# Moving the maximum's split, the scaled y and the fp8 bias to GpSimd, with all stack transfers on SyncE

## What is computed

```python
x = x + _layernorm(_L0_attn_ref(_layernorm(x), ...))   # 16 heads of 8, softmax attention, fp32
x = x + _layernorm(_L0_ffn_ref(_layernorm(x), ...))    # fp8 GEMM and a bias, bf16
x = x + _layernorm(_L1_attn_ref(_layernorm(x), ...))   # gated linear recurrence and an MLP
x = x + _layernorm(_L1_ffn_ref(_layernorm(x), ...))    # 8 experts of capacity 100
```

```python
scores = jnp.einsum('bhqd,bhkd->bhqk', q, k) / SCALING
att = jax.nn.softmax(scores, axis=-1)
...
x_q = (x.astype(jnp.float32) / s_in).astype(jnp.float8_e4m3fn)
y = jnp.dot(x_q.astype(jnp.float32), k_q.astype(jnp.float32), preferred_element_type=jnp.float32)
y = (y * (s_in * s_k)).astype(dtype) + bias
```

## Time and profile before

| | us |
|---|---|
| median of three runs (lowest, highest) | 1607.09 (1601.43, 1607.19) |
| span of the profiled execution, first to last instruction | 1596.0 |
| PE busy in it, matmul records | 1221.0 (77%) |
| DVE busy | 1231.6 (77%) |
| ACT busy | 976.0 (61%) |
| POOL busy | 839.4 (53%) |

### The profile page before, as it was taken

One profiled execution on the slowest core, in us unless ns is written; L12 is line 12 of the kernel. 1 busy time (PEld: TensorE's weight loads), 2 busy tenths in 40 slices (PEclk: granted clock), 3 DMA queues, 4 the chain that ended last, 5 costly groups with the idle time before them and its releaser, 6 DMA issues.

```text
span 1596.0 us, 25182 instructions
## 1 busy us (share of the span) xinstructions
PE 1221.0 (77%) x6480; PEld 465.6 (29%) x6480; DVE 1231.6 (77%) x2629; ACT 976.0 (61%) x1621; POOL 839.4 (53%) x1051
## 2 busy tenths in 40 slices
PE   1488888888798788798788888755887777887763
PEld 0022222222132222222222222122454444454442
DVE  2577789889779779778878887334688989989873
ACT  0067677777567677667667777434767566567630
POOL 5124355556455545545535543354377676677663
PEclk9979999999889999979989999676999999999976
DMA  2133023112202102102012020000000000000000
GB/s 42 24 81 47 19 31 48 33 15 49 48 1 47 37 12 47 31 18 47 20 29 47 8 35 2 0 1 0 1 7 7 14 7 7 13 7 7 14 7 20
DMA packets 46973, 37.10 MB, mean 23 GB/s; under 512 B 8080, under 2 KB 44816, under 8 KB 46864
## 3 DMA queue, kind: packets, MB, share of 16 engines
q1 hardware_dynamic: 42256, 29.65, 9.8%
q0 software_dynamic: 4608, 6.32, 2.5%
HBM read 6.04 MB, written 4.19 MB: 6 GB/s over the span
## 4 chain that ended last, share of the span: by engine, by line
PE 36%; DVE 22%; issue 16%; POOL 11%; ACT 8%; SPq 3%; DMA 3%; DVEq 1%; ACTq 0%; POOLq 0%
PE bank L218 13%; PE bank L202 11%; ACT probs L361 5%; DVE neg_max L505 5%; PE bank L226 3%; DVE probs L1061 3%; SPq L640 3%; DMA k_stack<-k_parts 2%; DVE probs L930 2%; PE bank_pair L189 2%; PE bank L287 2%; PE bank L749 2%; POOL probs L1171 1%; POOL rs_x L1104 1%; PE bank_pair L741 1%
## 5 line engine op out<-in xcount | busy, mean ns | idle before, releaser
L361 ACT ACTIVATE probs<-bank 128x512 f32<-128x512 f32 x1024 | 577.0, 598 | 261.0 <-PE bank L202 237.9
L505 DVE TENSOR_REDUCE neg_max<-bank_pair 128x2 f32<-128x1024 f32 x512 | 611.7, 1216 | 146.6 <-PE bank_pair L189 142.3
L202 PE MATMUL bank<-q_stack,k_stack 50*128 50x512 bf16 x1024 | 353.9, 409 | 119.6 <-ACT probs L361 119.3
L218 PE MATMUL bank<-probs,v_pad 128*32 128x512 f32 x2048 | 295.5, 652 | 0.0
L189 PE MATMUL bank_pair<-k_stack,q_stack 48*128 48x512 bf16 x1024 | 236.8, 407 | 48.0 <-DMA k_stack<-k_parts 24.8
L202 PEld LDWEIGHTS bank<-q_stack,k_stack 50*128 50x128 bf16 x1024 | 82.0, 93 | 549.4 <-ACT probs L361 487.7
L741 PE MATMUL bank_pair<-probs,w_gates 128*128 128x512 f32 x256 | 129.2, 652 | 20.5 <-DVE probs L1061 17.7
L1061 DVE SCALAR_TENSOR_TENSOR probs<-v_pad,conv_w,probs 128x512 f32<-128x512 f32 x96 | 98.1, 1061 | 6.3 <-ACT probs L893 5.6
L741 PE MATMUL bank_pair<-probs,w_in 128*128 128x512 f32 x128 | 65.1, 633 | 29.7 <-ACT probs L893 26.9
L1171 POOL TENSOR_TENSOR probs<-probs 128x1024 f32<-128x1024 f32 x16 | 37.8, 2360 | 90.1 <-DVE probs L1083 90.1
L189 PEld LDWEIGHTS bank_pair<-k_stack,q_stack 48*128 48x128 bf16 x1024 | 52.6, 96 | 85.9 <-DVE neg_max L505 49.1
(11 more groups left out here) (224 smaller groups left out, 2199.5 us busy)
## 6 DMA issues: line engine op xcount, KB each, us to landing
q_stack<-q_parts SPq DMA_DIRECT2D x192, 64.0 KB
k_stack<-k_parts POOLq DMA_DIRECT2D x96, 64.0 KB, 4.3
k_stack<-k_parts SPq DMA_DIRECT2D x96, 64.0 KB
x_all<-in_z_dram SPq DMA_DIRECT2D x16, 256.0 KB, 2.8
out_dram<-x_all SPq DMA_DIRECT2D x16, 256.0 KB, 2.3
q_stack<-max_rows SPq DMA_DIRECT2D x64, 8.0 KB
w_gates<-in_w_gates_dram SPq DMA_DIRECT2D x1, 512.0 KB, 3.7
w_in<-in_w_in_dram SPq DMA_DIRECT2D x1, 256.0 KB, 2.8
```

The lines of the kernel that those rows point to most:

```text
L202: nc.tensor.matmul(st_ps[h][:, :], k_stack[par][rows, p, c * P:(c + 1) * P], q_stack[par][rows, p, :], start=True, stop=True).then_inc(s[" ...
L218: mm = nc.tensor.matmul(acc[32 * g:32 * g + 32, :], v_pad[bpar][:, kc, 4 * a + g, :], probs[:, (a % 2) * 4 * C + g * C + kc, :], start=(t ...
L361: nc.scalar.activation(probs[:, (p // 2 % 2) * 4 * C + (2 * (p % 2) + h) * C + c, :], st_ps[h][:, :], ACT.Exp, scale=SCALE).then_inc(s["ex ...
L505: nc.vector.tensor_reduce(neg_max[j // 4][:, c, j % 4, :], score_ps[c % 2][:, :, :], AX_X, ALU.max, negate=True).then_inc(s["max_read"], 1)
```

## The change

- `y_scaled` goes from VectorE's slot 0 to the front of GpSimd's step, as a tensor_scalar with two operands (times the scale, times 1.0). VectorE's first grid operation waits for it by a new semaphore, `scaled_ready`.
- `f_b` goes from VectorE's slot 4 to GpSimd, behind the first norm.
- The split of the maxima goes to GpSimd: half 1 behind `f_b`, half 0 behind q's split.
- SyncE issues all 24 stack transfers; GpSimd issues none.
- GpSimd's casts in `split` get a second operand, and the first residual's subtraction and multiplication become one two-operand tensor_scalar for each of four chunks (`normed`), with one small negation before them.

```diff
-    STACK_DMAS = 3 * SPLIT
-    KSTACK_DMAS = SPLIT
+    STACK_DMAS = 4 * SPLIT
...
         def side(slot):
-            for at, half, off in ((5, 1, 0), (13, 0, 1)):
-                if slot == at and live(i, off):
-
-                    n = 2 * (i + off) + half
-                    m = neg_max[half][:, :, :, :].rearrange("p c j s -> p c s j")
-                    wait(dve, s["max_read"], 16 * (n + 1))
-                    wait(dve, s["maxT_ps"], n)
-                    nc.vector.tensor_copy(max_parts[:, :, :, 0], m).then_inc(s["max_split"], 1)
-                    wait(dve, s["max_split"], 2 * n + 1)
-                    nc.vector.tensor_tensor(max_parts[:, :, :, 1], m, max_parts[:, :, :, 0], ALU.subtract)\
-                        .then_inc(s["max_split"], 1)
...
-            if slot == 4 and live(i, -2):
-                b = i - 2
-                wait(dve, s["ffn_read"], b + 1)
-                wait(dve, s["x2_step"], 10 * b)
-                nc.vector.tensor_tensor(f_b[:, :, :], f_bf[:, :, :],
-                                        consts["ffn_bias"][:, :].unsqueeze(1).to_broadcast([P, C, D]), ALU.add)\
-                    .then_inc(s["ffn_biased"], 1)
...
-                wait(dve, s["y_step"], 4 * (b + 1))
-                nc.vector.tensor_scalar(y_scaled[:, :], y_bf[:, :, :].rearrange("p c d -> p (c d)"),
-                                        consts["s_in_inv"][:, 0:1], None, ALU.mult).then_inc(q, 1)
-                wait(dve, q, 10 * b + 1)
+                wait(dve, s["scaled_ready"], b + 1)
...
-        if live(i, 1):
-
-            b = i + 1
-            wait_apart(gp, s["k_lo"], 2 * (b + 1), past_wait)
-            wait_apart(gp, s["st_ready"], 64 * b - 64, past_wait)
-            for r, part in enumerate(K_PART):
-                gp.dma_start(k_stack[1 - par][64 + HD * r:64 + HD * (r + 1), :, :], k_parts[64:128, part, :])\
-                    .then_inc(s["kstack_ready"], 16)
...
+        def normed(dst, src, neg_mean, scale, done):
+            for c in range(C):
+                TS(dst[:, c, :], src[:, c, :], neg_mean[:, c:c + 1], scale[:, c:c + 1], ALU.add, ALU.mult)\
+                    .then_inc(done, 1)
+
+        def split_max(half, b):
+            n = 2 * b + half
+            m = neg_max[half][:, :, :, :].rearrange("p c j s -> p c s j")
+            wait_apart(gp, s["max_read"], 16 * (n + 1), past_wait)
+            wait_apart(gp, s["maxT_ps"], n, past_wait)
+            nc.gpsimd.tensor_copy(max_parts[:, :, :, 0], m).then_inc(s["max_split"], 1)
+            wait_apart(gp, s["max_split"], 2 * n + 1, past_wait)
+            TT(max_parts[:, :, :, 1], m, max_parts[:, :, :, 0], ALU.subtract).then_inc(s["max_split"], 1)
...
-            TS(parts[:, 1, :], rest[:, :], 1.0, None, ALU.mult).then_inc(s[n + "_lo"], 1)
+            TS(parts[:, 1, :], rest[:, :], 1.0, 1.0, ALU.mult, ALU.mult).then_inc(s[n + "_lo"], 1)
...
-                for h in range(halves):
+                for h in range(2):
```

More of the change, by code:

```diff
@@ L242, in side_product @@
             if slot == 2 and live(i, -2):
-                wait(pe, s["quant_step"], 10 * (i - 2) + 5)
+                wait(pe, s["quant_step"], 9 * (i - 2) + 4)
                 wait_misc_free(pe, i, "yT")
@@ L413, in side @@
                 wait(dve, s["zres_step"], 3 * (b + 1))
-                wait(dve, s["x1_step"], 5 * b)
+                wait(dve, s["x1_step"], 8 * b)
                 nc.vector.tensor_tensor(att[:, :, :].rearrange("p c d -> p (c d)"), misc[:, :],
@@ L426, in side @@
                 b = i - 2
-                wait(dve, q, 10 * b + 2)
+                wait(dve, q, 9 * b + 1)
                 nc.vector.tensor_scalar(y_grid[:, :], y_grid[:, :], 2.0 ** -6, 1.5 * 2.0 ** 20, ALU.max, ALU.mult)\
@@ L431, in side @@
                 b = i - 2
-                wait(dve, q, 10 * b + 3)
+                wait(dve, q, 9 * b + 2)
                 nc.vector.tensor_tensor(y_sum[:, :], y_scaled[:, :], y_grid[:, :], ALU.add).then_inc(q, 1)
@@ L435, in side @@
                 b = i - 2
-                wait(dve, q, 10 * b + 4)
+                wait(dve, q, 9 * b + 3)
                 wait(dve, s["yT_ps"], b)
@@ L474, in between @@
                 b = i - 2
-                wait(dve, q, 10 * b + 6)
+                wait(dve, q, 9 * b + 5)
                 nc.vector.tensor_scalar(y_absmax[:, :], y_absmax[:, :], 464.0, 464.0, ALU.max, ALU.subtract)\
@@ L479, in between @@
                 b = i - 2
-                wait(dve, q, 10 * b + 7)
+                wait(dve, q, 9 * b + 6)
                 nc.vector.tensor_scalar(y_absmax[:, :], y_absmax[:, :], 1e30, 1e30, ALU.mult, ALU.mult)\
@@ L484, in between @@
                 b = i - 2
-                wait(dve, q, 10 * b + 9)
+                wait(dve, q, 9 * b + 8)
                 wait(dve, s["x2_step"], 10 * b)
@@ L489, in between @@
                 b = i - 1
-                wait(dve, s["x1_step"], 5 * (b + 1))
+                wait(dve, s["x1_step"], 8 * (b + 1))
                 wait(dve, s["y_step"], 4 * b)
@@ L528, in x_of @@
             return x_all[:, b, :].rearrange("p (c d) -> p c d", c=C)
+        def normed(dst, src, neg_mean, scale, done):
[10 more added lines that the diff above has]
+            TT(max_parts[:, :, :, 1], m, max_parts[:, :, :, 0], ALU.subtract).then_inc(s["max_split"], 1)
+        if live(i, -2):
+            b = i - 2
+            wait_apart(gp, s["y_step"], 4 * (b + 1), past_wait)
+            wait_apart(gp, s["quant_step"], 9 * b, past_wait)
+            TS(y_scaled[:, :], y_bf[:, :, :].rearrange("p c d -> p (c d)"), consts["s_in_inv"][:, 0:1], 1.0,
+               ALU.mult, ALU.mult).then_inc(s["scaled_ready"], 1)
         if live(i, 2):
@@ L553, in pool @@
             TT(zn[:, :, :], centred[:, :, :], per_token(t(5)), ALU.mult).then_inc(s["zn_ready"], 1)
+        if live(i, -2):
+            b = i - 2
+            wait_apart(gp, s["ffn_read"], b + 1, past_wait)
+            wait_apart(gp, s["x2_step"], 10 * b, past_wait)
+            TT(f_b[:, :, :], f_bf[:, :, :], consts["ffn_bias"][:, :].unsqueeze(1).to_broadcast([P, C, D]), ALU.add)\
+                .then_inc(s["ffn_biased"], 1)
+        if live(i, 0):
+            split_max(1, i)
         if live(i, -1):
@@ L609, in pool @@
             split("q", q_parts, q_rest)
+        if live(i, 1):
+            split_max(0, i + 1)
         if live(i, -1):
@@ L634, in sync @@
             wait_apart(sp, s["st_ready"], 64 * b - 64, past_wait)
-            for done, parts, stack, order, halves in ((s["q_lo"], q_parts, q_stack[1 - par], Q_PART, 2),
-                                                      (s["k_lo"], k_parts, k_stack[1 - par], K_PART, 1)):
+            for done, parts, stack, order in ((s["q_lo"], q_parts, q_stack[1 - par], Q_PART),
+                                              (s["k_lo"], k_parts, k_stack[1 - par], K_PART)):
                 wait_apart(sp, done, 2 * (b + 1), past_wait)
-                for h in range(halves):
+                for h in range(2):
                     for r, part in enumerate(order):
```

19 lines of the change are left out of this document (8 added, 11 removed).

## The result

| | before | after |
|---|---|---|
| median of four runs, us (lowest, highest) | 1607.14 (1601.43, 1609.51) | 1649.68 (1644.05, 1659.76) |
| span of the profiled execution, us | 1596.0 | 1658.0 |
| mean granted clock of TensorE in it | 0.913 | 0.888 |
| start of the last exponential of the first phase, us | 1027.6 | 1095.8 |
| time at 1.2 GHz before 1000 us | 113 | 205 |

What follows compares the result with a forecast made beforehand. No engine fills the step; VectorE comes nearest and counts only where the chain of waits runs on it. The terms -14.4 + 6.7 - 3.3 + 2 = -9.0 us gave a median of 1598 us, range 1578 to 1624.

Steps and rivals of the forecast that it cites:

- Half 1, -14.4: Slot 5: splitting on GpSimd beside VectorE's reciprocal saves cast, subtraction and their stretches, letting max_t start earlier: -14.4 us.
- Half 0, +6.7: Slot 13: max_t waits longer for the split on GpSimd, +6.7 us; bounds 0 and 32.
- It loses 0.42 x 16: Slot 13: split before max_t takes 0.98 us in place of 0.56, losing 0.42 in each of 16 steps.
- y_scaled, -3.3: Step start: 1.16 us leaves VectorE's chain, the wait for GpSimd leaves 0.3 saved in 11 steps: -3.3 us.
- All transfers on SyncE, +2: Stack transfers: one queue for all 24, middle of -4.5 and +7.5 rounded up: +2 us; bounds -4.5 and +37.
- The bound from 72 GB/s: Stack transfers: 91 GB/s for 2.7 us, then 72, landed at +22.4 and late in slow early steps: +7.5 us.
- The rival of the slow queue: Next batch's first product at p = 3 waits for k's last transfer, under some 85 GB/s: 1633 us; chance 0.20.
- f_b, casts, normed: 0: f_b leaves VectorE's slot 4, off the chain; casts and normed free GpSimd where it waits for VectorE: 0 us.
- The split took 0.21 and 0.25 us, not 1.04: Rival, slots 5 and 13: each small split operation costs 1.04 us on GpSimd: 1637 us; chance 0.12.
- the casts got cheaper: Rival, GpSimd: second operand does nothing, cast and y_scaled cost 1.51 us each, grid 1.4 late: 1616 us; chance 0.07.
- VectorE wasn't the bound everywhere: Rival, whole step: VectorE bounds everywhere, so all 44.8 us taken off it count: 1562 us; chance 0.08.
- 8 us as what can be told: Whole kernel's time: about 0.5%, 8 us, was taken as what can be told from no change.

Runs made afterwards that it cites:

- e17: Kernel before with half 1's split, two-operand casts, normed and f_b on GpSimd, and all 24 transfers on SyncE: 1588.1 us, ratio 0.991.
- e8: Changed kernel with the split of half 0 back on VectorE, all 24 transfers still on SyncE: 1627.1 us, ratio 1.012.
- e10: Changed kernel with half 0's split on VectorE and only 18 transfers, all on SyncE (k's upper half not sent): 1561.7 us, ratio 0.971.
- e11: Kernel before without GpSimd's six transfers, SyncE's 18 as before (k's upper half not sent): 1588.2 us, ratio 0.986.
- e2: Kernel before with all 24 stack transfers on SyncE, nothing else moved: 1615.7 us, ratio 1.011.
- e3: Changed kernel with GpSimd issuing six transfers again, behind y_scaled, and half 0's split back on VectorE: 1603.9 us, ratio 1.000.
- e16: Kernel before with half 1's split, two-operand casts, normed and f_b on GpSimd, transfers as before: 1590.8 us, ratio 0.993.
- e5: Changed kernel, but SyncE sends a transfer only when the one three before it has landed: 1726.4 us, ratio 1.068.
- e9: e8 with an empty SyncE instruction ahead of each of the 24 transfers: 1617.6 us, ratio 1.004.
- e18: e16 with the split of half 0 added on GpSimd, transfers as in the kernel before: 1628.3 us, ratio 1.019.
- e14: Kernel before with half 1's split and y_scaled on GpSimd, casts of the parts still one-operand: 1601.8 us, ratio 0.997.

## Why the prediction was wrong

By differences of ratios the way from before to after is: half 1, casts, f_b and one queue together -14 us (e17), y_scaled +34 (e8), half 0 +22 (after), in all +42. The forecast had -12.4, -3.3 and +6.7.

- **Half 1, -14.4.** Right in direction and mechanism (-23 alone): the stretched operations went, and max_t came 1.2 us after the maximum. In the changed kernel itself it shows only in the steps whose stacks land early. From the rule of the Trainium skill, "SBUF — State Buffer", section "Who interferes with whom", I had drawn that VectorE's stretches would only move to other operations. A part did: the small operations on y_absmax grew by 3.4 us in all (longest 0.94 us, 0.56 before), where 9.2 us of stretch went. The first grid operation got 3.9 us shorter (longest 0.43, 2.45 before), so the sum hides it: 1189.2 us of VectorE against 1186.8 worked out without any new stretch.
- **Half 0, +6.7.** The step that failed is "It loses 0.42 x 16". The gap was right (0.96 us in place of 0.50) and so was the idle time, 6.1 to 7.6 us. What was missing is what the gap does: the granted clock falls behind it in half of the loop's steps or more, and the landing moves. The term measured 22 to 37 us. My upper bound of 32 was for slow operations, which they are not.
- **y_scaled, -3.3.** The step failed by its sign, and measured +34 between e17 and e8. Its own arithmetic was right: 0.69 us, and VectorE waits 10.3 us for it in 14 waits where 14.5 us of its own work stood. The row in the kernel after, 0 to 1100 us, in which 7.2 of the 10.3 fall:

```profile
L420 DVE TENSOR_SCALAR y_grid<-y_scaled 128x512 uint32<-128x512 uint32 x14 | 6.0, 426 | 7.2 <-POOL y_scaled L491 7.2
```

  What it costs comes by the transfers. Between e17 and e8 they are the same 24 on the same queue, and the packets go from 84 and 65 ns to 119 and 96, the landing in the even batches from +19.3 to +22.8. Where no landing is last it cost nothing that shows (e10 against e11). The prediction added GpSimd's order and the transfers as independent terms, and that is the second step that failed.
- **All transfers on SyncE, +2.** By itself it came to -3 in e17 and to +17 by ratio, +8 by medians in e2, within its bounds; beside y_scaled it was +19 (e8 against e3). The bound from 72 GB/s (landed at +22.4) is what the changed kernel shows, +22.8. But its +7.5 counted the late landing in the early steps alone, where the even batches of the loop have it too, with 2.9 to 3.2 us of waiting each. I took the middle of the bounds, and priced a late landing at the wait alone, with nothing for the clock behind it. The rival of the slow queue named the place, the mechanism and the point of decision (+19.9; the runs show +19.4), and its 1633 left out the clock, and half 0's share. The rule of the Trainium skill, "DMA: Bandwidth & Descriptors", section "Issuing engines are not separate DMA queues", that several issuers save only the issue time, agrees with e16 and e17. In e8 the same bytes land 1.8 us later than in e3 and the kernel is 19 us slower, and no run tells how much of that is issue time.
- **f_b, casts, normed: 0.** Right for each alone within what the runs tell; both together are open (e16).
- **The rivals.** The split took 0.21 and 0.25 us, not 1.04; the casts got cheaper; VectorE wasn't the bound everywhere: it lost 42 us of work and the kernel got slower.
- **8 us as what can be told** was too fine. Runs of one kernel scatter by 1.2% around their median, and a job's ratio is good to 0.3 to 1.0%.

Open: why the packets of the same transfers take 65 to 84 ns in one kernel and 96 to 120 in another. A queue of waiting transfers belongs to it (e5), spacing of 0.72 us doesn't cure it (e9), and y_scaled or half 0 on GpSimd brings it on (e17 to e8, e16 to e3 and to e18), though y_scaled beside half 1 alone did not (e14). In batch 8 y_scaled has ended 2.1 us after the first issue, and GpSimd is then idle to about +12 in e17 and in e8 alike; the packets still differ. No run shows what in them does it. Nor did any run keep the clock up over the same waits, so its share of the loss is read from the traces, not tested by itself.

## What to carry to other kernels

A term that is only idle time is too small where TensorE is busy most of a step (48 of 57 us here): read what the granted clock does behind the waits that the kernel already has, and price a new wait with it. Where a transfer lands within a microsecond or two of its use, it couples every other edit to itself, so price edits at both landings, and don't add them up one by one. Try the parts of such a change singly: here half 1 with the casts gives 0.986, the whole 1.026.

## What the runs showed that I had not expected

- A wait of 0.52 us ahead of max_t is followed by 3.4 us at 1.2 GHz in seven of ten steps (e18), one of 2.9 us by a stretch with a mean clock of 0.57 over 12 us (after).
- The same transfers of 64 KB between partitions go at 101 GB/s in one kernel and 72 in another. With three under way at most they go at 59 (e5), and 3.4 us pass from the first issue to the fourth.
- A second operand makes a GpSimd cast of 512 elements 2.4 times as fast: 0.62 us for 1.51.
